# Three split buffers, earlier mask rows and reordered super-block ends in a six-pass graph kernel

## The reference

```python
def _L0_gnn_ref(input, wavelets, wavelets_inv, W1, f1, W2, f2):
    def _gwnn_layer(features, wavelets, wavelets_inv, W, filt):
        return wavelets @ (filt[:, None] * (wavelets_inv @ (features @ W)))
    h1 = jax.nn.relu(_gwnn_layer(input, wavelets, wavelets_inv, W1, f1))
    return _gwnn_layer(h1, wavelets, wavelets_inv, W2, f2)
def _L1_gnn_ref(x, adj, beta):
    norm2 = jnp.linalg.norm(x, axis=1, keepdims=True)
    cos = beta * (x @ x.T) / (norm2 @ norm2.T + 1e-07)
    P = jax.nn.softmax(cos + (1.0 - adj) * -1000000000.0, axis=1)
    return P @ x
def _L2_gnn_ref(states, adj, W_msg, b_msg, W_ih, W_hh, b_ih, b_hh):
    msg = jax.nn.relu((adj @ states) @ W_msg.T + b_msg)
    return _gru_cell(msg, states, W_ih, W_hh, b_ih, b_hh)
def _L3_gnn_ref(h, adj, W_self, W_neigh):
    deg = jnp.clip(jnp.sum(adj, axis=1, keepdims=True), 1.0)
    return h @ W_self + (adj @ h / deg) @ W_neigh
x = _layernorm(x + _L0_gnn_ref(x, adj, adj, W1, f1, W2, f2))
x = _layernorm(x + _L1_gnn_ref(x, adj, beta))
x = _layernorm(x + _L2_gnn_ref(x, adj, W_msg, b_msg, W_ih, W_hh, b_ih, b_hh))
x = _layernorm(x + _L3_gnn_ref(x, adj, W_self, W_neigh))
```

## Time and profile before

| | us |
|---|---|
| median of 3 runs (1713.45 to 1720.19) | 1717.4 |
| the profiled execution | 1712.72 |
| its span, first to last instruction | 1710.9 |
| PE busy in the span | 1650.5 (96%) |
| DVE, ACT, POOL busy | 1377.6, 1236.7, 235.4 |
| bytes moved, mean rate | 461.61 MB, 270 GB/s |

### The profile page before, as it was taken

The page is one execution under the profiler, slowest core; times in us unless marked ns, Lnnn a source line. Parts: engine busy times, 40 slices in busy tenths (PEclk is TensorE's granted clock), DMA queues, the critical chain, the costliest instruction groups (busy, mean ns, idle before and its releaser), DMA issues.

```text
span 1710.9 us, 22249 instructions
## 1 busy us (share of the span) xinstructions
PE 1650.5 (96%) x8530; PEld 1376.0 (80%) x8530; DVE 1377.6 (81%) x1518; ACT 1236.7 (72%) x1251; POOL 235.4 (14%) x258
## 2 busy tenths in 40 slices
PE   7999999999999999978999999999899999999996
PEld 6888888888888887757999999999778767767885
DVE  6888887788878977776877878788788887787897
ACT  6776766676767766867787778787767777676775
POOL 0000000000000000166333333333330000000000
PEclk9999999999999999998999999999999999999998
DMA  9999999899989997963433344433569957848995
GB/s 393 381 375 370 377 340 373 292 370 368 360 297 383 370 364 275 331 232 144 149 139 122 134 148 148 149 143 127 210 198 357 348 178 249 292 163 287 354 332 170
DMA packets 63136, 461.61 MB, mean 270 GB/s; under 512 B 6672, under 2 KB 10928, under 8 KB 11312
## 3 DMA queue, kind: packets, MB, share of 16 engines
q1 hardware_dynamic: 63024, 460.14, 72.7%
HBM read 458.00 MB, written 2.11 MB: 269 GB/s over the span
## 4 chain that ended last, share of the span: by engine, by line
PE 84%; DVE 8%; ACT 4%; DMA 2%; issue 2%; POOL 0%; DVEq 0%; SPq 0%; ACTq 0%; POOLq 0%
PE ps L1183 18%; PE ps L1174 18%; PE ps L1177 18%; PE ps L1266 6%; DVE aL L794 4%; PE ps L1281 3%; PE ps L1283 3%; PE ps L1282 3%; PE ps L1251 3%; PE ps L1253 3%; PE ps L1252 3%; ACT aH L483 2%; DMA raw<-adjT 2%; DVE ptL L976 1%; PE ps L1213 1%
## 5 line engine op out<-in xcount | busy, mean ns | idle before, releaser
L794 DVE TENSOR_TENSOR aL<-raw,aH 128x2048 fp32r<-128x2048 f32 (+1 forms) x364 | 826.9, 2275 | 178.1 <-ACT aH L483 175.3
L483 ACT ACTIVATE aH<-raw 128x2048 fp32r<-128x2048 f32 (+1 forms) x364 | 689.9, 1899 | 260.5 <-PE ps L1177 173.0
L1174 PE MATMUL ps<-aH,yH 128*128 128x512 f32 x1472 | 408.4, 399 | 12.5 <-ACT aH L483 12.3
L1183 PE MATMUL ps<-aL,yH 128*128 128x512 f32 x1472 | 399.2, 393 | 12.2 <-DVE aL L794 12.2
L1177 PE MATMUL ps<-aH,yL 128*128 128x512 f32 x1472 | 395.4, 390 | 0.0
L1183 PEld LDWEIGHTS ps<-aL,yH 128*128 128x128 f32 x1472 | 273.7, 188 | 81.7 <-DVE aL L794 26.3
L1174 PEld LDWEIGHTS ps<-aH,yH 128*128 128x128 f32 x1472 | 271.5, 188 | 76.9 <-issue 19.4
L1177 PEld LDWEIGHTS ps<-aH,yL 128*128 128x128 f32 x1472 | 276.6, 188 | 58.8
L976 DVE TENSOR_TENSOR ptL<-ps,ptH 128x512 fp32r<-128x512 f32 x256 | 176.6, 690 | 87.9 <-ACT ptH L617 85.4
L617 ACT ACTIVATE ptH<-ps 128x512 fp32r<-128x512 f32 x192 | 114.3, 595 | 83.8 <-PE ps L1266 78.0
L414 POOL TENSOR_SCALAR raw<-raw 128x2048 f32<-128x2048 f32 x64 | 122.3, 1912 | 260.9 <-ACT raw L531 260.5
(11 more groups left out here) (146 smaller groups left out, 1675.8 us busy)
## 6 DMA issues: line engine op xcount, KB each, us to landing
raw<-adjT SPq DMA_DIRECT2D x364, 1024.0 KB, 5.9
raw<-adj SPq DMA_DIRECT2D x30, 2048.0 KB, 8.3
raw<-adj SPq DMA_DIRECT2D x4, 1024.0 KB, 6.8
kept<-adjT SPq DMA_DIRECT2D x4, 1024.0 KB, 12.0
xT<-norms SPq DMA_DIRECT2D x1, 2048.0 KB, 6.9
out<-xrow SPq DMA_DIRECT2D x8, 256.0 KB, 4.8
xrow<-x_rows SPq DMA_DIRECT2D x1, 1024.0 KB, 14.7
xrow<-x_rows SPq DMA_DIRECT2D x1, 768.0 KB, 9.1
```

Of the source, the lines that this page charges most:

```text
L483: ins = nc.scalar.activation(a_tiles(q, t)[0][:, cols], a_source(q, t)[:, cols], ACT.Copy)
L794: ins = dve.tensor_tensor(low[:, cols], a_source(q, t)[:, cols], high.bitcast(F32)[:, cols], ALU.subtract)
L1174: pe.matmul(b, block(yH, k), high[:, c], start=(k == 0), stop=False)
L1183: ins = pe.matmul(b, block(yH, k), low[:, c], start=False, stop=(k == NB - 1))
```

## The change

A third buffer for split tiles is added. It lies in `kept`: in its last quarter in passes 0 to 3, in its second quarter in passes 4 and 5. For that room, tile 16 is no longer split once (three such tiles stay), and tiles 8 and 40 are no longer kept raw (24 and 56 stay). The mask of super block 1 is loaded into and made in the two quarters of `kept` where its masked scores then go ("in place"), so its rows need not wait for `rowbuf`; ACT sums the first of them before the first exponentials, and POOL makes their addends earlier. The last `sum_batch` of a super block moves behind the first `turn_batch` and `scores` of the next, and ACT's `o_copy` moves behind the first `turned_high` and one `exponent`. At the end of the attention ACT splits tile 4 of pass 4 ahead of the last `o_copy`. Some side work is hung on later tiles. The unit norms are staged in `xT` instead of `kept`.

```diff
-    SPLIT_ONCE = (16, NB + 3, NB + 6, NB + 9)
-    KEPT = tuple(range(8, TILES, 16))
+    SPLIT_ONCE = (NB + 3, NB + 6, NB + 9)
+    KEPT = (24, 56)
+    ABUFS = 3
...
-    UNIT_AT, X1_AT = (13, 15, 18, 20), (25, 27)
-    X2_LOW_AT = {4: 5, 5: 7, 6: 12, 7: 13}
+    UNIT_AT, X1_AT = (14, 16, 19, 21), (25, 27)
+    X2_LOW_AT = {4: 5, 5: 7, 6: 17, 7: 18}
...
+        spare = {early: [sb_over(f"spare{part}{early}", [D, HALF], F32R, kept_base + (3 if early else 1) * N * 4 + at)
+                         for part, at in (("H", 0), ("L", HALF * 4))] for early in (0, 1)}
...
-            slot = buf_place[q, t] % 2
+            slot = buf_place[q, t] % ABUFS
+            if slot == ABUFS - 1:
+                return [part[:, :] for part in spare[int(q < 4)]]
...
+        def mask_row(sbi, r):
+
+            return rows_of[2 + r] if sbi == 1 else rowbuf[:, r, :]
...
+            for r in range(2):
+                sp.wait_ge(tile_used, gn(3, SPLIT_ONCE[2]) + 1 if r == 0 else 4 * TILES)
+                sp.dma_start(mask_row(1, r), adj_rows[2 + r]).then_inc(row_landed[r], 16)
...
-            for r in range(2):
-                sp.wait_ge(m_ready, masks_of_row(NSB - 1, r))
-                for at in first_after_rows[2 * r:2 * r + 2]:
-                    load_tile(*at)
+            for at in first_after_rows:
+                sp.wait_ge(m_ready, masks_of_row(NSB - 1, ring_place[at] % RING // 2))
+                load_tile(*at)
...
             stage_unit(1, 0)
+            for h in range(2):
+                mask_bias(1, 0, h, 5 + h)
             normalise(1, HBK + 1)
             low_of_x(4, X1_BY_ACT + 1)
             stage_unit(1, 1)
-            for h in range(2):
-                mask_bias(0, h, 5 + h)
...
             high_of_x(1, X1_BY_ACT + 1)
+            for h in range(2):
+                degrees(2, h)
...
-                    if k == 0 and before:
-                        o_copy(sbi - 1)
                     if k not in HIGH_BY_DVE:
                         turned_high(sbi, k)
                     if k + NBATCH - first_r1 < NCH and before:
                         exponent(sbi * 2 + 1, 2 * parity + 1, k + NBATCH - first_r1)
+                    if k == 0 and before:
+                        o_copy(sbi - 1)
...
             super_block(NSB - 1, 1, 0, True)
+            split_high(4, EARLY_TILES)
             o_copy(NSB - 1)
...
-                        if u == 11:
+                        if u == 12:
                             for i in range(3, SCALE_STEPS):
                                 scale_step(i, 0, HBK, 0, NB // 2)
...
                     if k >= 1:
                         sum_batch(sbi, k - 1, before)
+                    elif before:
+                        sum_batch(sbi - 1, NBATCH - 1, sbi >= 2)
                     if k == 2 and before:
                         turn_sums(sbi - 1, second)
-                sum_batch(sbi, NBATCH - 1, before)
```

More of the change, by code:

```diff
@@ L170, in build @@
         assert NB * 6 <= early_at["W2"][0]
-        uT = kept[0:NB, 2, 0:D]
+        uT = xT[0:NB, 0:D]
         S_BANKS, PT_BANKS, O_BANK, OT_BANK = (0, 2), (4, 5), 6, 7
@@ L183, in a_tiles, with after_attention @@
                 return onceH[i][:, :], onceL[i][:, :]
-            slot = buf_place[q, t] % 2
+            slot = buf_place[q, t] % ABUFS
+            if slot == ABUFS - 1:
+                return [part[:, :] for part in spare[int(q < 4)]]
             return aH[:, slot, :], aL[:, slot, :]
         def a_before(q, t):
-            if is_split_once(q, t) or buf_place[q, t] < 2:
+            if is_split_once(q, t) or buf_place[q, t] < ABUFS:
                 return None
-            return buf_tiles[buf_place[q, t] - 2]
+            return buf_tiles[buf_place[q, t] - ABUFS]
+        def after_attention(eng, q, t):
+            if buf_place[q, t] % ABUFS == ABUFS - 1:
+                eng.wait_ge(s_ready, NB * NCH)
+            else:
+                eng.wait_ge(pt_ready, (NSB - 1) * NBATCH)
         def a_source(q, t):
@@ L350, in _ @@
             sp.wait_ge(urow_landed, 16)
-            for sbi in range(1, NSB):
+            for sbi in range(2, NSB):
                 for r in range(2):
                     sp.wait_ge(m_ready, masks_of_row(sbi - 1, r))
-                    sp.dma_start(rowbuf[:, r, :], adj_rows[sbi * 2 + r]).then_inc(row_landed[r], 16)
-            for r in range(2):
-                sp.wait_ge(m_ready, masks_of_row(NSB - 1, r))
-                for at in first_after_rows[2 * r:2 * r + 2]:
-                    load_tile(*at)
+                    sp.dma_start(mask_row(sbi, r), adj_rows[sbi * 2 + r]).then_inc(row_landed[r], 16)
+            for at in first_after_rows:
+                sp.wait_ge(m_ready, masks_of_row(NSB - 1, ring_place[at] % RING // 2))
+                load_tile(*at)
             sp.wait_ge(s_ready, NB * NCH)
@@ L409, in stage_unit, with mask_bias @@
                 pool.tensor_tensor(wL[:, r, :], tmp, wH[:, r, :].bitcast(F32), ALU.subtract).then_inc(bw_ready, 1)
-            def mask_bias(r, h, nth):
+            def mask_bias(sbi, r, h, nth):
                 pool.wait_ge(deg_done, nth)
-                t = rowbuf[:, r, h * HALF:(h + 1) * HALF]
+                t = mask_row(sbi, r)[:, h * HALF:(h + 1) * HALF]
                 pool.tensor_scalar(t, t, -1.0, MASK, ALU.add, ALU.mult).then_inc(bias_ready, 1)
@@ L421, in _ @@
             normalise(1, X1_BY_ACT)
-            mask_bias(0, 0, 1)
-            mask_bias(1, 0, 2)
+            mask_bias(0, 0, 0, 1)
+            mask_bias(0, 1, 0, 2)
             normalise(1, X1_BY_ACT + 1)
@@ L476, in split_high @@
                 before = a_before(q, t)
-                if q == 4 and t < 2:
-                    act.wait_ge(pt_ready, (NSB - 1) * NBATCH)
+                if q == 4 and t < ABUFS:
+                    after_attention(act, q, t)
                 elif before is not None:
@@ L658, in _ @@
                     exponent(r, r, c)
-                    if r == 1 and c >= 2:
-                        degrees(2, c - 2)
             super_block(0, 0, 2, False)
@@ L732, in _ @@
             for t in range(EARLY_TILES, TILES):
-                split_high(4, t)
-                if t == 6:
+                if t > EARLY_TILES:
+                    split_high(4, t)
+                if t == 10:
                     root(3, EARLY_LN, NB)
-                if t in (8, 10):
+                if t in (13, 15):
                     act.wait_ge(rstd_ready, 4)
-                    normalise(X2_BY_POOL + (t - 8) // 2, x_by_act)
-                if t in (11, 12):
-                    high_after_sums(X2_BY_POOL + t - 11)
+                    normalise(X2_BY_POOL + (t - 13) // 2, x_by_act)
+                if t in (16, 17):
+                    high_after_sums(X2_BY_POOL + t - 16)
                 if 8 <= t < 8 + 2 * BK and t % 2 == 0:
@@ L787, in split_low @@
                 before = a_before(q, t)
-                if q == 4 and t < 2:
-                    dve.wait_ge(pt_ready, (NSB - 1) * NBATCH)
+                if q == 4 and t < ABUFS:
+                    after_attention(dve, q, t)
                 elif before is not None:
@@ L947, in mask_chunk @@
                     dve.wait_ge(urow_landed, 16)
-                    corr = row[:, c * CH:(c + 1) * CH]
+                    corr = rows_of[2 * (sbi % 2) + r][:, c * CH:(c + 1) * CH] if sbi != 1 else rowbuf[:, r, c * CH:(c + 1) * CH]
                     dve.tensor_scalar(corr, xT[:, c * CH:(c + 1) * CH], epsu[:, rb:rb + 1], 1.0, ALU.mult, ALU.add)
@@ L959, in mask_chunk @@
                     dve.wait_ge(bias_ready, rb * 2 + c // (NCH // 2) + 1)
-                dve.tensor_tensor_reduce(row[:, c * CH:(c + 1) * CH], S2[m % 2], rowbuf[:, r, c * CH:(c + 1) * CH],
+                dve.tensor_tensor_reduce(row[:, c * CH:(c + 1) * CH], S2[m % 2], mask_row(sbi, r)[:, c * CH:(c + 1) * CH],
                                          1.0, LOWEST, ALU.add, ALU.max, cmax[:, r, c:c + 1]).then_inc(m_ready, 1)
```

12 lines of the change are left out of this document (7 added, 5 removed).

## The result

The changed kernel takes 1705.86 us in the median of 5 runs (1704.20 to 1708.15), the kernel before 1717.4 (1713.45 to 1721.65): a ratio of 0.9935, 95% interval 0.9915 to 0.9955. The forecast was 1705.3. The two profiled executions differ by less, 1712.72 against 1705.78, where 1700.6 was forecast. The windows of the changed kernel show where to look (columns as in the earlier trace rows).

What follows compares the result with a forecast made beforehand. PE, busy 1650.5 of 1710.9 us, was taken as the bound. Terms -6.0 - 4.2 - 1.2 - 1.1 + 0.4 = -12.1 us gave 1700.6 profiled and, with 4.7 carried over, a median of 1705.3, range 1695 to 1713.

Steps and rivals of the forecast that it cites:

- Ends of super blocks: Between super blocks, PE's wait for DVE's parts of batch 15 goes: 0.4 us per end, 15 ends, -6.0 us.
- Entry to super block 0: Early rows remove DVE's 9.13 us wait; POOL is late next, and row 3's mask moves by about 4.2 us: -4.2.
- Half rows: Super block 0's second half row waits for the last split, at most 3.1 us later: +0.4 us, bounds 0 and +3.1.
- POOL's waits further on swallow such a shift: Step for super block 0's half rows: POOL's later waits absorb their delay, so the cost stays near 0.
- Pass 3: PE's 1.17 us wait at 679.38 for DVE goes, with layer-norm steps a tile later and a third buffer: -1.2 us.
- Entry to pass 4: The 0.62 us wait goes by ACT's early split of tile 4, and half of the 1.07 us wait: -1.1 us.
- Costed at nothing: Tile 16's extra splits, the net five extra 1 MB loads and the two 3.7 us stretches in passes 4 and 5: 0.
- The copy is waited for once: Rival at super block ends: ACT's exponent delays the bank's copy, giving back 6.0 us: 1711.3 us, chance 0.17.
- The clock did fall in the shorter wait: Rival at the entry to super block 0: shorter waits also halve PE's clock, 2.7 us less gain: 1708.0 us, chance 0.12.
- a granted clock of 1.00 after them: Sign at the entry to super block 0: PE's waits each under 4 us, with full clock behind them.
- The third buffer did not reach the two stretches: Rival: the third buffer also bridges the two 3.7 us stretches in passes 4 and 5: 1697.9 us, chance 0.18.
- Loading did not become the bound: Slower rival: loads at 2.83 us per tile bind long runs of tiles and cost 30.1 us: 1735.4 us, chance 0.05.

Runs made afterwards that it cites:

- e_ends: The kernel before with only the reordered ends of super blocks (PE's last product and ACT's copy moved): 1707.94 us against 1715.85, ratio 0.9953.
- e_rows: The kernel before with only super block 1's rows loaded early, masked in place and made earlier by POOL: 1713.38 us, ratio 0.9984.
- e_pass3: The changed kernel with the side work of pass 3 on its old places: 1705.54 us, ratio 0.9927 of before.
- e_mask: The changed kernel with POOL's first addend of super block 1's second row put ahead of two normalised chunks: 1703.40 us, ratio 0.9929 of before.
- e_two: The changed kernel with two split buffers in place of three, nothing else changed: 1707.56 us, ratio 0.9948 of before.
- e_best: The changed kernel with every tile one raw buffer further on and POOL's first addend of super block 1's second row earlier: 1702.41 us against 1718.97, ratio 0.9903.
- e_ring: The changed kernel with every tile one raw buffer further on (the ring begins at buffer 1): 1707.71 us, ratio 0.9936 of before.
- e_two4: The changed kernel with two split buffers, tile 16 split once again and tiles 8 and 40 kept raw again: 1705.03 us, ratio 0.9921 of before.

## Why the prediction was right

The forecast of the time was right to 0.6 us, and its two largest terms hold for the reasons given. Four smaller amounts were missed: the half rows by +1.1 us, pass 3 by +1.3, the entry to pass 4 by -1.5, the ends by -1.0. These misses nearly cancel, so that the time came out so close is luck.

- **Ends of super blocks, -6.0:** measured -5.5 over thirteen and -1.0 at the fourteenth, and some 0.5 more at the first (-0.7 in e_ends); -7.1 alone (e_ends). The period went from 30.1 to 29.7 as reckoned from the starts of the matmuls. The fifteen ends are not alike, though: the one before the last super block, where no scores stand between, had two waits, 0.35 and 1.07 us, and has one of 0.8 now. The copy's margin held; without ACT's half the edit costs 6.8 us over the same stretches. PE's timeline before, at that end:

```profile
1233.16 0.36 PE L1281 MATMUL ps<-ptH,yH 128*128 128x256 f32 x1 [1.07 <-DVE ptL L976]
```

- **Entry to super block 0, -4.2:** measured -4.2 from the norm on, but some 0.5 of it is the first end: -3.7 alone (e_rows). That POOL is next is shown by DVE's 2.81 us and by the kernels with the earlier addend, where that wait is gone.
- **Half rows, +0.4:** the step "POOL's waits further on swallow such a shift" failed, and the path was another. The line of the earlier trace rows holds the second to the fourth half row; the first left at 728.87. The second left at 733.99, 4.8 us ahead of the first score (738.79), and in the changed kernel at 742.50, 1.7 us ahead of it (744.18): 3.1 us later, the bound that was named. SP's timeline, before and changed:

```profile
733.99 0.33 SPq L341 DMA_DIRECT2D raw<-adj  x1
```

```profile
742.50 0.33 SPq L357 DMA_DIRECT2D raw<-adj  x1
```

ACT sums the second and third half row before it takes the root that DVE needs for the norms. Now it waits for both (ACT's timeline), and DVE for the root (its own):

```profile
747.64 1.92 ACT L550 ACTIVATE raw<-raw 128x2048 f32<-128x2048 f32 x1 [0.57 <-DMA raw<-adj]
...
751.56 1.91 ACT L550 ACTIVATE raw<-raw 128x2048 f32<-128x2048 f32 x1 [1.92 <-DMA raw<-adj]
```

```profile
754.24 0.35 DVE L873 RECIPROCAL s<-s 128x32 f32<-128x32 f32 x1 [1.25 <-ACT s L541]
```

Before, ACT had no such wait and stood idle for 1.09 us ahead of the root. That swallows 1.1 of the 2.5 us, and the rest, 1.4, is nearly all of the 1.5 by which the norm comes later (+0.5 to +1.3 in the other profiles with that ring). The waits of POOL that were counted on come behind the norm and could not swallow it. The price lay in the range given, 0 to 3.1.

- **Pass 3, -1.2:** nothing came of it. The wait of 1.17 us shrank to 0.68, but the whole pass took as long as before (174.91 against 174.80), and e_pass3 shows that the move makes no difference.
- **Entry to pass 4, -1.1:** -2.6. The term was undersized: the tile that ACT splits early is worth 1.3 with the restart behind the waits, where the one wait of 0.62 was counted, and the moved steps 1.1, where half of a wait was. A third wait there, 1.45 us at 1272.66, does not stand in the prediction's rows, and it stays (1.46 us).
- **Costed at nothing:** the gated unit's stretches, unchanged. The extra loads: pass 1 is 1 us slower in the mean with them, pass 2 evener with the third buffer.
- **The rivals.** The copy is waited for once (0.8 us), not at each end. The clock did fall in the shorter wait, after 2.12 us and not at the wait before the second row, so the sign "a granted clock of 1.00 after them" failed. It cost nothing here: e_pass3, with the same ring and the same wait of 2.1 us, kept full speed and took 60.42 us from the norm on, against 60.37. There PE waits 3.12 us before the second row, where the changed kernel waits 1.48: POOL was the limit in both. Where POOL is out of the way (e_mask), a fall costs 1.5. The third buffer did not reach the two stretches. Loading did not become the bound with three buffers; with two, e_two shows ACT waiting for most loads of pass 2. PE's window in e_pass3 behind its wait of 2.1 us:

```profile
778.70:781.70 3.00, 2.96 (x22) 2.85 (x23) 2.97 (x5) 2.15 (x4) 2.74 (x6) 1.00 0.02 5
```

Where the profiled executions stood to the medians was taken over as a plain 4.7 us. That was right for the median, for a reason the prediction did not name: the profile of before had a fast pass 0. For the profile itself the forecast, 1700.6, missed by 5.2.

## What to carry to other kernels

Move work on two engines together when one hands over to the other: one half of a reordering can cost what the whole of it wins. Before a stretch is credited with a gain, look for the engine that is next (here POOL, by the rows of its list): while it is the limit, time lost ahead of it can vanish in the wait for it. When a load moves, follow it into every list in which something waits for it; here ACT's sums and not POOL's addends carried the delay on. Compare profiles by stretches between fixed instructions, so that the chance of one stage is not booked as an effect of another.

## What the runs showed of the hardware

Loads in pass 0 came at 367 to 392 GB/s in the first 100 us from execution to execution, with the same tiles loaded in the same order, and the pass took 182 to 189 us. The windows of the two extremes of the rate, e_two and e_rows:

```profile
0.00:100.00 100.00, 90.20 (x384) 73.79 (x385) 79.07 (x41) 69.53 (x43) 0.20 (x4) 1.00 0.99 392
```

```profile
0.00:100.00 100.00, 87.34 (x360) 68.41 (x361) 73.50 (x39) 65.09 (x40) 0.20 (x4) 1.00 0.97 367
```

The span of pass 0, 7.6 us, is nearly that of the five runs of before (8.2 us), so it may be most of the scatter of the times; no kernel was profiled twice to show it. It bounds what a comparison of single executions can tell. What sets the rate was not tried.

TensorE's clock did not answer to the length of a wait alone. A wait of 2.1 us before the same product stands in eleven profiles: after it the clock fell to half in three (the changed kernel, e_rows, e_mask) and stayed at full speed in eight, e_best among them. Before the second row six profiles have a wait of 3.1 to 3.5 us: after it the clock fell in two (3.44 us in e_ring, 3.42 in e_two) and stayed in four (3.49 us in e_two4). The Trainium skill (TensorE: Matmul & The Clock Gate, Part 1: The HAM clock gate) says that the number of slow matmuls at the start of a kernel differs between runs of that kernel. The profiles here are of different kernels, so no run shows it for one.
